# Attention on one core: the values of the unit behind are multiplied between the two pairs of scores

## The chip, the cores and the metric

The kernel runs on one core of a Trainium2 chip. The metric is the device time of one execution in microseconds (us), lower is better. The kernel before takes 2456.95 us, the median of three runs (2456.72 to 2460.13).

## The reference

Two layers act on x of 2 x 2048 tokens with 256 channels. The change is in the attention of the first layer, which has 16 heads of 16 channels and is causal. Cut to what matters:

```
Qr = rope(h @ W_q.T), Kr = rope(h @ W_k.T), V = h @ W_v.T      # per head
scores  = einsum('bhqd,bhkd->bhqk', Qr, Kr) * DH ** -0.5
scores  = where(causal, finfo.min, scores)
pattern = softmax(scores, axis=-1)
heads   = einsum('bhqk,bhkd->bhqd', pattern, Vh)
out     = heads.transpose(0, 2, 1, 3).reshape(b, t, d) @ W_o.T
```

Before it stand a layer norm and the projections, behind it a gated sum, a top-1 expert layer, a second layer with a Toeplitz mix, and a routed expert layer. None of these is touched.

## The kernel before, in words

The program runs its parts one after the other: `projections`, `attention`, `output_projection`, `top1_experts`, `layer1`, `routed_experts`, `combine`. Each has one instruction stream for each engine, written out by hand, with semaphores between them. TensorE works through its stream in the order written: an instruction that waits holds up all behind it.

**Stages and units.** Attention has 8 stages of 4 heads each. A stage has 40 units (c, j): c is a chunk of 512 queries (0 to 3), j a block of 128 keys, up to the diagonal (4(c+1) blocks for chunk c). The units with j >= 4c, 16 of the 40, are on the diagonal; their first columns are left out (`lo`), so their four heads are 512, 384, 256 and 128 queries wide in turn. The 24 others are full, 512 wide. Unit numbers n run from 0 to 39 here; chunks begin at n = 0, 4, 12 and 24, diagonal units are n = 0 to 3, 8 to 11, 20 to 23 and 36 to 39.

For a unit the engines do this:

- TensorE, `scores` (line 819): for each head h one matmul, keys by queries, into one of three banks `p_s` (NSCORES = 3, line 608). It waits until the exponential three places earlier has been taken out of its bank.
- ScalarE (ACT), `exponentials` (line 914): one exponential for each head, from `p_s` to `probs`, which has room for three units.
- GpSimd (POOL), `mask` (line 770): on a diagonal unit, zeroes the upper half of a 128x128 block of each head, once its exponential is done; `diag_masked` is raised behind the fourth.
- TensorE, `values` (line 833): four matmuls of 32 rows of output each, one a head, which add values times `probs` into `p_o`. It first waits for the fourth exponential of its unit, or on the diagonal for the fourth mask. At j = 0 it also waits for `o_taken`, since `p_o` starts anew: ACT copies the finished chunk out (`take_o`, line 920), behind the four exponentials of the new chunk's first unit.

**Maxima.** The softmax needs row maxima, found one stage ahead by separate matmuls (`maximum_products`, lines 216 and 219): 80 maxima in a stage, each of two heads, for a 128-query tile and up to 512 keys, into one of two places `p_m`; on the diagonal each of the two matmuls is followed by a small one that adds the mask. VectorE (DVE) reduces them (line 227). A maximum waits until the reduction two before it is done. The table MAXIMA (line 653) says how many maxima of the next piece go behind the first pair of scores of each unit and how many behind the second, for example (2, 1) or (1, 0): 18 units of 40 have none behind their second pair, 20 have one, 2 have two. Behind units 5, 19, 23 and 31 TensorE turns finished maxima into rows (line 842), and behind the fourth unit of each chunk (j = 3) it turns an output chunk (line 849), which DVE then divides (lines 975 and 977). The last stage has no next one, so its maxima end with unit 17.

**Order on TensorE** (`stage`, line 852): for each unit, scores of heads 0 and 1; the maxima of this place; scores of heads 2 and 3; the values of the unit behind (n - 1); the maxima of this place. The unit behind unit 0 is the last one of the stage before. The code shown next has these functions.

Of the kernel before, what the change touches and what calls it, by code (L numbers as in the profile page):

```python
# [91 lines left out]
def first(i):  # L92
    return isinstance(i, int) and i == 0
# [504 lines left out]
def attention(nc, a, k):  # L598
# [7 lines left out]
    with ExitStack() as stack:  # L606
# [71 lines left out]
        def maxima_of(n, pair, more):  # L678

            u0 = 2 * MAX_LEAD + sum(map(sum, MAXIMA[:n])) + (MAXIMA[n][0] if pair else 0)  # L680
            return [u for u in range(u0, u0 + MAXIMA[n][pair]) if u < NMAX or more]

        def maxima_turned_at(s, n, more):

            c, following = TURN_MAXIMA.get(n, (None, False))
            if c is None or following and not more:
                return None
            return (s + 1 if following else s), c

        def output_at(s, n):  # L690

            c, j = units[n]
            if j != AFTER_TURN_O or not c and first(s):
                return None
            return (s, c - 1) if c else (s - 1, CPS - 1)
# [12 lines left out]
        def m_bank(x):  # L708

            return M_AT[x] % 2  # L710

        def s_bank(x, buf):

            return (M_SHIFT * buf + S_AT[x]) % NSCORES
# [3 lines left out]
        def wait_m_bank(pe, s, x, more):  # L718

            i = M_AT[x] - 2  # L720
            if i < 0:
                what, which = M_ORDER[i]
                which -= NMAX if what == "max" else CPS
                if first(s):
                    what, which = "max", 2 * MAX_LEAD + i
            else:
                what, which = M_ORDER[i]
            if first(s) and (what, which) == ("out", -1):
                what, which = M_ORDER[i - 2]
            if not more and what == "max" and which >= NMAX:  # L730
                while what == "max" and which >= NMAX:
                    i -= 2
                    what, which = M_ORDER[i]
            if what == "max":
                pe.wait_ge(k.max_taken, NMAX * s + which + 1)
            else:
                pe.wait_ge(att_ready, CPS * s + which + 2)

        def wait_s_bank(pe, s, x, more):

            i = S_AT[x] - NSCORES
            if i < 0 and first(s):
                if i + NSCORES < 2:
                    pe.wait_ge(max_rows_ready, i + NSCORES + 1)
                return
            if not more and S_ORDER[i][0] == "rows" and S_ORDER[i][1] >= CPS:
                i -= NSCORES
            what, which = S_ORDER[i]
            if what == "rows":
                pe.wait_ge(max_rows_ready, CPS * (s if i >= 0 else s - 1) + which + 1)  # L750
            else:
                pe.wait_ge(probs_ready, HG * UNITS * s + which + 1 - (0 if i >= 0 else HG * UNITS))

        with nc.Block(no_gpsimd_drain=True) as block:
# [55 lines left out]
            def _(pe):  # L810
                def maximum(s, buf, u, at_bank):
                    maximum_products(nc, k, qa[buf], ka[buf], u, p_m[:, at_bank, :, :]).then_inc(k.max_scores, 1)

                def scores(s, buf, n, h, more):
                    c, j = units[n]
                    lo = max(0, j - TPC * c) * P
                    x = ("exp", HG * n + h)
                    wait_s_bank(pe, s, x, more)
                    nc.tensor.matmul(p_s[:, s_bank(x, buf), lo:CH], ka[buf][0:QROWS + SPLIT, h, j * P:(j + 1) * P],  # L819
                                     qa[buf][0:QROWS + SPLIT, h, c * CH + lo:(c + 1) * CH],  # L820
                                     start=True, stop=True).then_inc(scores_ready, 1)

                def values(s, buf, n):
                    c, j = units[n]
                    lo = max(0, j - TPC * c) * P
                    if n in diag_no:
                        pe.wait_ge(diag_masked, DIAGS * s + diag_no[n] + 1)
                    else:
                        pe.wait_ge(probs_ready, HG * (UNITS * s + n) + HG)
                    if j == 0 and (c or not first(s)):  # L830
                        pe.wait_ge(o_taken, CPS * s + c)
                    for h in range(HG):
                        last = nc.tensor.matmul(p_o[VW * h:VW * (h + 1), lo:CH], va[buf][:, j, VW * h:VW * (h + 1)],  # L833
                                                probs[:, (buf * UNITS + n) % NPROBS, h, lo:CH], start=j == 0, stop=j == TPC * (c + 1) - 1)
                    last.then_inc(probs_used, 1)

                def turn_maxima(n, at_bank):

                    pe.wait_ge(max_parts_ready, n + 1)
                    rows = p_s[:, at_bank, :].bitcast(BF16)  # L840
                    for i in range(TPC):
                        last = nc.tensor.transpose(rows[0:SPLIT * HG, i * P:(i + 1) * P],
                                                   max_parts[:, i, :, :].rearrange("p s h -> p (s h)"), k.identb[:, :])
                    last.then_inc(max_turned, 1)

                def turn_outputs(s, c, at_bank):
                    pe.wait_ge(o_taken, CPS * s + c + 1)
                    for u in range(TPC):
                        last = nc.tensor.transpose(p_m[:, at_bank, 0, u * P:(u + 1) * P], o_sb[:, u * P:(u + 1) * P],
                                                   k.ident[:, :])  # L850
                    last.then_inc(o_turned, 1)

                def stage(s, buf, more, loads):
                    nbuf = (buf + 1) % NBUF
                    for n, (c, j) in enumerate(units):
                        if j == 0:
                            pe.wait_ge(max_placed[c % 2], PLACED * (CPS // 2 * s + c // 2 + 1))
                            if c == 0 and not first(s):
                                pe.wait_ge(ones_set, NBUF - 1)
                        for pair in range(2):  # L860
                            scores(s, buf, n, 2 * pair, more)
                            scores(s, buf, n, 2 * pair + 1, more)
                            if pair:

                                if n:
                                    values(s, buf, n - 1)
                                elif not first(s):
                                    values(s - 1, (buf - 1) % NBUF, UNITS - 1)
                            for u in maxima_of(n, pair, more):
                                if u == NMAX:  # L870
                                    pe.wait_ge(stage_loaded[nbuf], 16 * LOADS * loads)
                                wait_m_bank(pe, s, ("max", u), more)
                                if u < NMAX:
                                    maximum(s, buf, u, m_bank(("max", u)))
                                else:
                                    maximum(s + 1, nbuf, u - NMAX, m_bank(("max", u)))
                        turned = maxima_turned_at(s, n, more)
                        if turned:
                            x = ("rows", CPS * TURN_MAXIMA[n][1] + TURN_MAXIMA[n][0])
                            wait_s_bank(pe, s, x, more)  # L880
                            turn_maxima(CPS * turned[0] + turned[1], s_bank(x, buf))
                        out = output_at(s, n)
                        if out:
                            x = ("out", c - 1)
                            wait_m_bank(pe, s, x, more)
                            turn_outputs(*out, m_bank(x))

                pe.wait_ge(k.stage0_loaded, 16 * LOADS)
                for u in range(EARLY, 2 * MAX_LEAD):
# [7 lines left out]
                    if ends_chunk(u):  # L897
                        turn_maxima(MAX_UNITS[u][0], MAX_UNITS[u][0])
                all_stages(pe, stage)
                values(NS - 1, (NS - 1) % NBUF, UNITS - 1)  # L900
                pe.wait_ge(att_ready, CPS * NS)
# [1642 lines left out]
```

## Time and profile before

| | |
|---|---|
| median of the runs | 2456.95 us |
| the profiled execution | 2465.7 us |
| its span, from first to last instruction | 2464.0 us |
| attention's units in it | about 225 to 1095 us |
| TensorE matmuls busy, whole span | 2207.4 us (90%) |
| VectorE, ScalarE, GpSimd busy | 1713.8, 1273.3, 877.2 us |
| exponentials, line 914, ScalarE | 1280, 596.4 us busy |
| reductions, line 227, VectorE | 628, 642.0 us busy |
| matmuls of values, line 833 | 2560 records, 301.8 us |
| matmuls of scores, line 819 | 1280 records, 352.0 us |

How to read it: a matmul's record lasts from its start to the end of its result, and the next one starts before that. So TensorE's busy time says that something was in it, not that it was full; what a step costs TensorE is the distance between the start of its first matmul and the start of what follows. A timeline line merges neighbours of one kind (x4) and starts at the first.

### The profile page before, as it was taken

To read this page: it belongs to the slowest core of one execution; us is meant where nothing else is said; L and a number is where in the kernel's file an instruction comes from. 1 tells how busy PE (TensorE), PEld (TensorE's weight loads), DVE (VectorE), ACT (ScalarE), POOL (GpSimd) and SP (SyncE) were. 2 spreads that over 40 slices of the span, in tenths; PEclk is the share of its full clock that TensorE was granted. 3 is DMA by queue.
4 is the path that set the end of the run, shared out by engine and by line. 5 is a ranking of instruction groups with operands and counts; after the bars stand their busy time and mean duration, and the time that the engine had idled before them with its cause. 6 is when DMAs were issued, how large, how long until landed. Compare 5 with 4: busy or idle time off the path is not lost. (4 is left out here: it accounts for less than half of the span.)

```text
span 2464.0 us, 38748 instructions
## 1 busy us (share of the span) xinstructions
PE 2207.4 (90%) x12968; PEld 1401.7 (57%) x12968; DVE 1713.8 (70%) x2750; ACT 1273.3 (52%) x2452; POOL 877.2 (36%) x1057
## 2 busy tenths in 40 slices
PE   7878999999999999979999599962999999999991
PEld 5752333333333333326777456642888888888881
DVE  8968787878788787816888778764455555555566
ACT  3332777777677777773333344421555555555552
POOL 4542321313121220213555413444345444445350
PEclk9986999999999999998999798875999999999996
DMA  6499004225050500012000100004544434444326
GB/s 211 141 209 120 19 8 64 35 37 70 3 70 2 70 2 2 1 58 76 0 0 0 34 1 18 35 33 158 180 142 138 144 133 137 169 157 142 133 74 218
DMA packets 129541, 199.84 MB, mean 81 GB/s; under 512 B 13712, under 2 KB 102416, under 8 KB 127952
## 3 DMA queue, kind: packets, MB, share of 16 engines
q1 hardware_dynamic: 112992, 143.93, 17.5%
q0 software_dynamic: 14544, 48.05, 10.9%
q10 hardware_dynamic: 1824, 5.52, 1.3%
q8 instruction: 105, 1.72, 0.3%
q14 instruction: 76, 0.62, 0.1%
HBM read 150.58 MB, written 46.49 MB: 80 GB/s over the span
## 5 line engine op out<-in xcount | busy, mean ns | idle before, releaser
L227 DVE TENSOR_REDUCE tile_max<-p_m 128x2 f32<-128x1024 f32 (+1 forms) x628 | 642.0, 1064 | 135.9 <-PE p_m L219 67.9
L914 ACT ACTIVATE probs<-p_s 128x512 f32<-128x512 f32 (+3 forms) x1280 | 596.4, 534 | 241.3 <-PE p_s L819 236.1
L2180 PE MATMUL p_up<-f_xT,f_w 128*128 128x512 f32 (+1 forms) x2304 | 464.4, 351 | 12.1 <-POOL f_w L2345 8.6
L2180 PEld LDWEIGHTS p_up<-f_xT,f_w 128*128 128x128 f32 x2304 | 368.6, 189 | 64.7 <-issue 14.3
L770 POOL TENSOR_SCALAR_AFFINE_SELECT probs<-probs 128x128 f32<-128x128 f32 x512 | 145.9, 294 | 700.8 <-ACT probs L914 692.2
L2345 POOL TENSOR_TENSOR f_w<-f_raw,f_w 128x1024 fp32r<-128x1024 f32 x96 | 233.3, 2437 | 374.4 <-ACT f_w L2233 374.4
L819 PE MATMUL p_s<-qa,ka 99*128 99x512 bf16 (+3 forms) x1280 | 352.0, 351 | 13.0 <-ACT probs L914 7.2
L216 PE MATMUL p_m<-ka,qa 96*128 96x512 bf16 (+1 forms) x1256 | 352.9, 363 | 11.1 <-DVE tile_max L227 5.0
L833 PE MATMUL p_o<-probs,va 128*32 128x512 f32 (+3 forms) x2560 | 301.8, 542 | 1.2 <-issue 0.9
L2195 PE MATMUL p_y<-f_w,f_hidden 128*128 128x256 f32 x1872 | 252.9, 281 | 15.0 <-DVE f_y L2307 14.1
L2195 PEld LDWEIGHTS p_y<-f_w,f_hidden 128*128 128x128 f32 x1872 | 238.1, 188 | 29.8 <-issue 21.6
L216 PEld LDWEIGHTS p_m<-ka,qa 96*128 96x128 bf16 x1256 | 108.2, 99 | 237.3 <-DVE tile_max L227 137.1
L2294 DVE SCALAR_TENSOR_TENSOR f_gate<-p_up,f_b,f_gate 128x512 f32<-128x512 f32 (+1 forms) x192 | 124.6, 649 | 168.3 <-ACT f_gate L2246 165.8
L819 PEld LDWEIGHTS p_s<-qa,ka 99*128 99x128 bf16 x1280 | 110.5, 98 | 223.3 <-ACT probs L914 141.5
L2298 DVE TENSOR_TENSOR f_hidden<-f_gate,f_hidden 128x512 fp32r<-128x512 f32 (+1 forms) x192 | 141.3, 736 | 118.7 <-ACT f_hidden L2251 110.8
L2246 ACT ACTIVATE f_gate<-p_up,f_b 128x512 f32<-128x512 f32 (+1 forms) x192 | 116.3, 606 | 155.5 <-PE p_up L2180 148.7
L1268 PE MATMUL p_e<-w_expert,c_hT 128*128 128x512 f32 x768 | 195.0, 404 | 0.0
L2251 ACT ACTIVATE f_hidden<-f_gate 128x512 fp32r<-128x512 f32 (+1 forms) x192 | 105.9, 552 | 159.9 <-DVE f_gate L2294 156.6
L1268 PEld LDWEIGHTS p_e<-w_expert,c_hT 128*128 128x128 f32 x768 | 140.6, 190 | 29.5
L2233 ACT ACTIVATE f_w<-f_raw 128x1024 fp32r<-128x1024 f32 x144 | 150.4, 1045 | 5.8 <-DMA f_raw<-in_W1b 3.9
L1706 PE MATMUL p_uv<-l_xnT,w_uv 128*128 128x512 f32 x256 | 112.8, 597 | 0.0
L536 PE MATMUL p_qk<-hT,wqkv 128*128 128x512 f32 x384 | 97.3, 413 | 13.0 <-DVE rot L397 13.0
(279 smaller groups left out, 2622.3 us busy)
## 6 DMA issues: line engine op xcount, KB each, us to landing
f_raw<-in_W1a SPq DMA_DIRECT2D x24, 1024.0 KB, 6.5
f_raw<-in_W1b SPq DMA_DIRECT2D x24, 1024.0 KB, 8.7
f_raw<-in_W SPq DMA_DIRECT2D x24, 1024.0 KB, 11.1
qk_scr<-parts SPq DMA_DIRECT2D x48, 256.0 KB, 2.8
qa<-qk_scr POOLq DMA_DIRECT2D x42, 256.0 KB, 15.9
ka<-qk_scr POOLq DMA_DIRECT2D x42, 256.0 KB, 17.6
v_scr<-wqkv_raw SPq DMA_DIRECT2D x32, 256.0 KB, 3.8
g_ys<-y_rows SPq DMA_DIRECT2D x16, 512.0 KB, 8.8
```

Of the source, the lines that this page charges most:

```text
L216: last = nc.tensor.matmul(out[:, hh, 0:width], qa[0:QROWS, hd, q0:q0 + P], ka[0:QROWS, hd, bank * CH:bank * CH + width], start=True, stop= ...
L227: return nc.vector.tensor_reduce(out=k.tile_max[:, 2 * hp:2 * hp + 2, i, bank], in_=products[:, :, 0:width], op=ALU.max, axis=AX.X)
L770: last = nc.gpsimd.affine_select(block_, block_, pattern=[[1, P]], compare_op=ALU.is_ge, fill=0.0, base=0, channel_multiplier=-1)
L819: nc.tensor.matmul(p_s[:, s_bank(x, buf), lo:CH], ka[buf][0:QROWS + SPLIT, h, j * P:(j + 1) * P], qa[buf][0:QROWS + SPLIT, h, c * CH + lo: ...
L833: last = nc.tensor.matmul(p_o[VW * h:VW * (h + 1), lo:CH], va[buf][:, j, VW * h:VW * (h + 1)], probs[:, (buf * UNITS + n) % NPROBS, h, lo: ...
L914: nc.scalar.activation(probs[:, (buf * UNITS + n) % NPROBS, h, lo:CH], p_s[:, s_bank(("exp", HG * n + h), buf), lo:CH], ACT.Exp, scale=DH ...
L1268: last = nc.tensor.matmul(out, hT[:, par, hp, kt, :], weights(wp, kt), start=(kt, wp, hp) == (0, HI, HI), stop=(kt, wp, hp) == (KT - 1, LO ...
L2180: last = nc.tensor.matmul(p_up[:, f % 2, ab, 0:size], w1[:, wh, ab * KT + kt, f * P:(f + 1) * P], xT[:, t % 2, xh, kt, 0:size], start=(kt, ...
L2195: last = nc.tensor.matmul(p_y[:, u, :], hidden[:, (FB * t + f) % NHID, hh, u * P:(u + 1) * P], w2[:, wh, f, :], start=(f, wh, hh) == (0, H ...
L2233: nc.scalar.activation(piece_part(q, HI), piece_raw(q, par), ACT.Copy).then_inc(w_high, 1)
L2298: nc.vector.tensor_tensor(hidden[:, (n - 1) % NHID, LO, 0:size], gate[:, f % 2, 0:size], hidden[:, (n - 1) % NHID, HI, 0:size], ALU.subtra ...
L2345: nc.gpsimd.tensor_tensor(piece_part(q, LO), piece_raw(q, t % 2), piece_part(q, HI), ALU.subtract).then_inc(w1_ready, 1)
```

## The change

In `stage` of TensorE's stream one condition is turned round. `values(n - 1)` stands behind the first pair of scores of unit n, ahead of the maxima of the first place, and no longer behind the second pair. Nothing is added or removed, and the streams of the other engines are the same.

```diff
@@ -860,7 +860,7 @@
                         for pair in range(2):
                             scores(s, buf, n, 2 * pair, more)
                             scores(s, buf, n, 2 * pair + 1, more)
-                            if pair:
+                            if not pair:
 
                                 if n:
                                     values(s, buf, n - 1)
```

**First place, TensorE, on the diagonal of chunk 1 in the first stage** (units 9 to 11, second pair of unit 9 to second pair of unit 11). p_s is scores, p_o values, p_m maxima. Before:

```order
L819 MATMUL p_s<-qa,ka 128x384 x2
L833 MATMUL p_o<-probs,va 32x512 x4
L819 MATMUL p_s<-qa,ka 128x256 x2
L216 MATMUL p_m<-ka,qa 128x512 x4
L819 MATMUL p_s<-qa,ka 128x256 x2
L833 MATMUL p_o<-probs,va 32x384 x4
L819 MATMUL p_s<-qa,ka 128x128 x2
L216 MATMUL p_m<-ka,qa 128x512 x2
L819 MATMUL p_s<-qa,ka 128x128 x2
L833 MATMUL p_o<-probs,va 32x256 x4
```

Now:

```order
L819 MATMUL p_s<-qa,ka 128x384 x2
L819 MATMUL p_s<-qa,ka 128x256 x2
L833 MATMUL p_o<-probs,va 32x384 x4
L216 MATMUL p_m<-ka,qa 128x512 x4
L819 MATMUL p_s<-qa,ka 128x256 x2
L819 MATMUL p_s<-qa,ka 128x128 x2
L833 MATMUL p_o<-probs,va 32x256 x4
L216 MATMUL p_m<-ka,qa 128x512 x2
L819 MATMUL p_s<-qa,ka 128x128 x2
```

The 384-wide values of unit 9 stood behind four matmuls of scores of unit 10 and its maxima; now they stand behind its first pair, which follows at once on the second pair of unit 9, since this unit has no maxima in its second place.

**Second place, TensorE, at the start of chunk 2** (from the first pair of unit 12; the four-in-a-row of scores are the second pair of one unit and the first of the next). Before:

```order
L819 MATMUL p_s<-qa,ka 128x512 x2
L216 MATMUL p_m<-ka,qa 128x512 x2
L819 MATMUL p_s<-qa,ka 128x512 x2
L833 MATMUL p_o<-probs,va 32x128 x4
L819 MATMUL p_s<-qa,ka 128x512 x2
L216 MATMUL p_m<-ka,qa 128x512 x2
L216 MATMUL p_m<-ka,qa 128x384
L219 MATMUL p_m<-masks,identb 128x128
L216 MATMUL p_m<-ka,qa 128x384
L219 MATMUL p_m<-masks,identb 128x128
L819 MATMUL p_s<-qa,ka 128x512 x2
L833 MATMUL p_o<-probs,va 32x512 x4
```

Now:

```order
L819 MATMUL p_s<-qa,ka 128x512 x2
L833 MATMUL p_o<-probs,va 32x128 x4
L216 MATMUL p_m<-ka,qa 128x512 x2
L819 MATMUL p_s<-qa,ka 128x512 x4
L833 MATMUL p_o<-probs,va 32x512 x4
L216 MATMUL p_m<-ka,qa 128x512 x2
L216 MATMUL p_m<-ka,qa 128x384
L219 MATMUL p_m<-masks,identb 128x128
L216 MATMUL p_m<-ka,qa 128x384
L219 MATMUL p_m<-masks,identb 128x128
L819 MATMUL p_s<-qa,ka 128x512 x4
L833 MATMUL p_o<-probs,va 32x512 x4
```

The values of unit 12 are the last line of the first piece, behind both pairs of unit 13 with its maxima between. In the second piece they are the fifth line, and only the first pair of unit 13 lies between the second pair of unit 12 and them; the last line there is the values of unit 13.

## Rows read from the trace of the kernel before

**Rows 1.** Busy time by stretch: attention, a stage's start, the last stage's tail

```profile
core 0: us, PE busy (x) PEld busy (x) DVE busy (x) ACT busy (x) POOL busy (x), PEclk, DMA share, GB/s
225.00:1095.00 870.00, 849.57 (x5746) 304.91 (x5744) 664.45 (x818) 622.74 (x1341) 192.16 (x579) 0.99 0.21 30
660.00:670.00 10.00, 5.90 (x33) 2.09 (x32) 4.72 (x5) 3.08 (x9) 1.96 (x7) 0.70 0.04 9
1064.00:1074.00 10.00, 8.73 (x52) 2.21 (x51) 4.88 (x10) 7.96 (x16) 0.00 (x0) 1.00 0.01 2
```

**Rows 2.** Timeline, two full units: start, us, engine, line, work, count, [idle before, releaser]

```profile
596.58 0.60 PE L819 MATMUL p_s<-qa,ka 99*128 99x512 bf16 x2
596.99 1.09 ACT L914 ACTIVATE probs<-p_s 128x512 f32<-128x512 f32 x2 [0.53 <-PE p_s L819]
597.10 1.06 PE L833 MATMUL p_o<-probs,va 128*32 128x512 f32 x8
598.10 0.61 PE L216 MATMUL p_m<-ka,qa 96*128 96x512 bf16 x2
598.54 0.60 PE L819 MATMUL p_s<-qa,ka 99*128 99x512 bf16 x2
598.75 2.36 DVE L227 TENSOR_REDUCE tile_max<-p_m 128x2 f32<-128x1024 f32 x2 [0.36 <-PE p_m L216]
...
599.53 0.59 PE L819 MATMUL p_s<-qa,ka 99*128 99x512 bf16 x2
```

**Rows 3.** Timeline, TensorE: the transpositions between two units

```profile
573.71 0.66 PE L849 MATMUL p_m<-ident,o_sb 128*128 128x128 f32 x4
...
574.20 0.60 PE L819 MATMUL p_s<-qa,ka 99*128 99x512 bf16 x2
...
639.87 0.60 PE L216 MATMUL p_m<-ka,qa 96*128 96x512 bf16 x2
...
640.73 0.60 PE L819 MATMUL p_s<-qa,ka 99*128 99x512 bf16 x2
```

**Rows 4.** Timeline, TensorE: the values of a 256-wide unit and what follows

```profile
582.94 0.64 PE L833 MATMUL p_o<-probs,va 128*32 128x256 f32 x8
...
583.51 0.60 PE L216 MATMUL p_m<-ka,qa 96*128 96x512 bf16 x2
```

**Rows 5.** Timeline, TensorE: start of the second stage and of the fifth

```profile
335.12 0.60 PE L819 MATMUL p_s<-qa,ka 99*128 99x512 bf16 x2
...
665.69 1.03 PE L819 MATMUL p_s<-qa,ka 99*128 99x512 bf16 x2 [4.10 <-issue]
```

**Rows 6.** Timeline: the last stage's tail, which has no maxima

```profile
1047.06 1.06 PE L833 MATMUL p_o<-probs,va 128*32 128x512 f32 x8
...
1071.75 0.82 PE L819 MATMUL p_s<-qa,ka 99*128 99x512 bf16 x3
1072.23 2.06 ACT L914 ACTIVATE probs<-p_s 128x512 f32<-128x512 f32 x4 [0.39 <-PE p_s L819]
1072.88 0.39 PE L819 MATMUL p_s<-qa,ka 99*128 99x512 bf16 x1 [0.32 <-ACT probs L914]
1073.20 1.07 PE L833 MATMUL p_o<-probs,va 128*32 128x512 f32 x8
...
1094.76 0.43 PE L833 MATMUL p_o<-probs,va 128*32 128x128 f32 x8 [0.30 <-POOL probs L770]
```

**Rows 7.** Groups by shape, attention: the exponentials of a 128-wide unit

```profile
L914 ACT ACTIVATE probs<-p_s 128x128 f32<-128x128 f32 x128 | 28.5, 275 | 19.2 <-PE p_s L819 16.5
```

**Rows 8.** Timeline: what follows a unit's exponentials, on POOL and on ACT

```profile
584.37 2.06 ACT L914 ACTIVATE probs<-p_s 128x512 f32<-128x512 f32 x4 [0.94 <-PE p_s L819]
...
586.29 0.63 ACT L920 ACTIVATE o_sb<-p_o 128x512 f32<-128x512 f32 x1
...
607.74 2.24 ACT L914 ACTIVATE probs<-p_s 128x512 f32<-128x512 f32 x4
...
610.05 0.29 POOL L770 TENSOR_SCALAR_AFFINE_SELECT probs<-probs 128x128 f32<-128x128 f32 x1 [0.19 <-ACT probs L914]
```

## The prediction

> **What bounds the kernel now.** I read the busy time by stretch first [rows 1]. Attention's units take 870 us, and in them TensorE's records cover 849.6 us, VectorE's 664.5, ScalarE's 622.7, at a granted clock of 0.99, so at the upper of TensorE's two levels, 2.4 GHz. Only TensorE can be the bound. But a record outlives its turn, so I go on to the timeline of TensorE and measure distances between starts [rows 2]. A pair of 512-wide scores, alone, costs 0.44 us; before values it costs 0.53 (596.58 to 597.10), so values cost a lead of 0.1; the four matmuls of values cost 1.00 (597.10 to 598.10); an unmasked maximum 0.44 (598.10 to 598.54); pair and masked maximum together 0.99 (598.54 to 599.53), so the masked one 0.55. Turning an output costs 0.49 (573.71 to 574.20); turning maxima 0.42, which is 639.87 to 640.73 less a maximum [rows 3].
>
> I price a whole stage with these. Scores and maxima scale with their width (384, 256 and 128 columns), and of values the 256-wide ones cost 0.57 [rows 4], so about 0.785 and 0.355 at 384 and 128. Scores: 28 units of 0.88 and 4 each of 0.66, 0.44 and 0.22 make 29.9 us. Values with their lead: 28 x 1.10 + 4 x (0.885 + 0.67 + 0.455) = 38.8. Maxima: 48 unmasked at 0.44 and 8 each at 0.55, 0.44, 0.33 and 0.22 make 33.4. Transpositions: 4 x 0.42 + 4 x 0.49 = 3.6 (one output a chunk). Sum 105.8 us. A stage lasts (665.69 - 4.10 - 335.12) / 3 = 108.8 us [rows 5]; the 4.10 is the idle time at the loop's turn. So TensorE is full but for 3.0 us a stage, and **any wait that the new order puts in front of it costs its full length**.
>
> **What the change does.** Work and its amount stay. Moved are 319 calls of values (40 a stage, but for the one behind the last unit), each past one pair of scores and the maxima of the first place. No transfer is moved, and no instruction of another engine. What changes is how much TensorE has to do between the second pair of scores of unit n and values(n), which needs all four exponentials of that unit. Before: first pair and maxima of unit n + 1, and its second pair too, and the second pair's wait for a bank already covers the fourth exponential. Now: the maxima behind n's second pair and one pair.
>
> **How long the exponentials take.** From the start of the second pair to the end of its second exponential: 0.41 (596.58 to 596.99) plus 1.09 for the two [rows 2], so 1.50. From there to a waiting matmul 0.06: in the tail the first of four exponentials starts at 1072.23, takes 0.60 (two take 1.09, four 2.06, so each further one adds 0.49) and so ends at 1072.83 and the waiting score starts at 1072.88 [rows 6]. So **values(n) can start 1.56 us after the second pair** of a full unit. Narrower ones: a 128-wide exponential takes 0.275 [rows 7] against 0.60, so two take about 0.44, and by straight line 0.66 and 0.87 at 256 and 384; the 0.41 falls to 0.28, 0.32 and 0.37 by the columns streamed. On the diagonal the mask follows: exponentials end at 609.98, the mask at 610.34, 0.36 more [rows 8]. That makes 1.92, 1.66, 1.40 and 1.14 us for 512, 384, 256 and 128.
>
> **What covers it.** Second pair 0.44, maxima behind it, next first pair 0.44, lead 0.1: 0.98 for a full unit without maxima there, 1.42 with one. The wait is the difference.
> - Full units (24): five without maxima or transposition (12, 13, 28, 30, 34) wait 0.58, 2.9 together; nine with 0.44 us of maxima (4, 6, 14, 16, 24, 26, 32, 33, 35) 0.14, 1.3; 18, 25 and 19 wait 0.36, 0.25 and 0.16; 7, 15 and 27, where an output is turned, 0.09 each; 17 and 29 0.03; 5 and 31 nothing. Sum **5.3**.
> - Diagonal units (16): unit 8 1.05; the 384-wide 1, 9, 21 1.01 each (1.66 less 0.33 + 0.22 + 0.1); the 256-wide 2, 10, 22 0.97 each; 0 and 20 0.50 each, 36 to 39 with 0.61, 0.57, 0.53 and 0.49; 11 0.05; 3 and 23 nothing. Sum **10.2**.
> - A wait that the diff does not show: values at j = 0 also need `o_taken`. ACT copies the output behind the fourth exponential and ends 0.49 us after it (586.92 against 586.43) [rows 8]. So units 0, 4, 12 and 24 come at 1.50 + 0.49 + 0.06 = 2.05: 0.13 more for unit 0 and 0.49 for the three others. Sum **1.6**.
> - The maxima: two in the first place and one in the second now have only 0.44 us of scores between them, since the values have gone. The first is reduced 0.65 + 1.18 us after it starts [rows 2], so the third may start at 1.89 and is ready at 0.88 + 0.44 = 1.32, 0.57 late. Where values would wait anyhow, part of it is hidden: 0.43 more at units 6, 16, 33, 0.57 at 31, 0.54 at 29, 0.2 at 14. Sum **2.6**. In return the values now stand between a turned output and the next maximum, which had waited for VectorE's division. That belongs to the 3.0 us of now, which I let go entirely.
>
> New stage: 105.8 + 5.3 + 10.2 + 1.6 + 2.6 = 125.5, so **+16.7 us**, seven times 117. Last stage: its first 18 units take their part, 7.5 + 1.1 + 1.0 less 18/40 of 3.0, +8.3. Then there are no maxima, and the time from values(18) to values(39) is 47.7 us now (1047.06 to 1094.76) [rows 6]. The new period is the exponentials' time plus the values': 13 x 1.56 + 0.49 + 2 x (1.92 + 1.66 + 1.40 + 1.14) for units 19 to 39, and 19.1 of values, 52.1 us: +4.4. At the first units of stages 1 and 5 TensorE runs at the lower level (0.70 granted in the mean of that stretch, 1.03 for two scores against 0.60 [rows 1, 5]), where its own work covers unit 0's wait: -1. Total 117 + 8.3 + 4.4 - 1 = **+129 us**. The profiled execution of 2465.7 us would take 2595; against the median, 2456.95, I forecast **2586 us**.
>
> The unknown sizes. The 0.41 was 0.48 in the tail (1071.75 to 1072.23) [rows 6]: on some 35 waits in 8 stages up to +20. The maxima's term lies between nothing (-20) and twice (+20). Without the wait for `o_taken`, -13. So 2553 to 2626.
>
> **The rivals.**
> 1. *Only long waits count.* The 0.09 to 0.58 of full units are no waits, because TensorE would be held up by VectorE in that same place whatever the order: DVE's reductions, 1.18 each, two a unit, are the next longest. Then diagonal and `o_taken` remain, (10.2 + 1.6 - 3.0) x 8 = +70: 2527 us. Against it: VectorE is busy only 76% of the stretch [rows 1].
> 2. *The clock falls.* With a wait in most units, TensorE might be granted the lower level for part of the time. If for a tenth, its work doubles there: 0.1 x 8 x 105.8 = +85, of which waits cover 0.1 x 8 x 19.7 = 16: +69, 2655 us. Against it the tail: TensorE waits there in every unit of 2.45 us for a bank (0.32 of it idle by its records), and the clock is 1.00 [rows 1, 6]. The Trainium skill (TensorE: Matmul & The Clock Gate, section "A second HAM failure mode: psum-queue depth-cycling") says that short, frequent idling of TensorE between groups of matmuls while it cycles through PSUM banks makes the clock swing between its levels. By that rule this rival would be the likeliest; this trace does not agree, with its 1.00.
> 3. *Faster.* The exponentials are done when values come up, and the 3.0 us a stage of present waits go, for values now part the turned output from the next maximum: -24, 2433 us. It decides at 0.98 us from second pair to last exponential. For it: probabilities come free earlier. Against it: two exponentials alone take 1.09 [rows 2].
> 4. *No difference.* The order is the same where it counts, or TensorE isn't the bound. The instructions' order above says that each call moved; the length of a stage against the sum of its work says that it is full [rows 5]: 2457 us.
>
> **How the numbers follow.** The forecast has 0.77, rival 1 0.09, rival 2 0.07, rival 3 0.04, rival 4 0.03. A range of 2525 to 2626 us takes in the forecast's bounds and rival 1 and leaves out the rest, with a little for sizes that I have missed. A measurement of this kernel can tell about 0.2%, 5 us. Faster 0.04, the same 0.03, slower 0.93.
>
> **What would show it.** In the profile of the changed kernel, TensorE's weight loads or matmuls of values (line 833) must wait for ScalarE (line 914), on the diagonal for POOL (line 770) and at chunk starts for the output copy (line 920), where before there was next to nothing; a stage must last about 125 us; distances from second pair to values must be 1.56 on full and 1.92 on 512-wide diagonal units; work between stays at 105.8. VectorE's and ScalarE's busy time must not change. The forecast is wrong if stages last under 115 us, if values start sooner than 1.5 us after the second pair, or if the granted clock in attention falls below 0.97.

## The result and the profile after

The changed kernel takes 2615.29 us (median of four, 2609.84 to 2618.61) against 2458.54 us of the kernel before beside it: a ratio of 1.0622, 95% interval 1.0599 to 1.0644, **156.8 us slower**. Forecast were 2586 us and +129. The profiled execution took 2618.59 us.

Nearly all of it lies in attention. The last values of the last stage start at 1246.04 us, before at 1094.76 [rows 6], 151.3 later, and the two profiled executions differ by 152.9 us (2618.59 against 2465.7). The first scores start at 225.63 in the changed kernel and at 225.66 before, so attention, from first scores to last values, takes 1020.4 us against 869.1. The same stretches as in [rows 1], columns as there: all of attention, a full stretch, the last stage's tail.

```profile
core 0: us, PE busy (x) PEld busy (x) DVE busy (x) ACT busy (x) POOL busy (x), PEclk, DMA share, GB/s
225.00:1246.00 1021.00, 887.08 (x5738) 302.49 (x5736) 667.45 (x818) 619.29 (x1341) 189.65 (x579) 0.99 0.18 25
340.00:440.00 100.00, 87.05 (x587) 31.14 (x588) 68.46 (x85) 60.06 (x136) 24.46 (x77) 1.00 0.32 43
1160.00:1240.00 80.00, 66.78 (x407) 18.62 (x407) 27.50 (x37) 56.21 (x119) 10.13 (x36) 1.00 0.00 1
```

VectorE's and ScalarE's busy time is what it was (664.5 and 622.7 in [rows 1]), the granted clock 0.99 as before. TensorE's records no longer fill the time. Where the second and the fifth stage start:

```profile
353.98 0.98 PE L819 MATMUL p_s<-qa,ka 99*128 99x128 bf16 x4
...
743.47 1.03 PE L819 MATMUL p_s<-qa,ka 99*128 99x512 bf16 x2 [3.46 <-issue]
```

The first row holds two pairs that merge: the last of the first stage, 128 wide and 0.11 us by the prediction's costs, and the first of the second stage, which so starts at 354.09. A stage lasts (743.47 - 3.46 - 354.09) / 3 = 128.6 us, against 108.8 before [rows 5] and 125.5 forecast. The view of the waits over attention's stretch says on whom TensorE now waits (engine and line, for whom, us in total, times, longest). PE are its matmuls; PEld are its weight loads. These overlap running matmuls (at 886.84 us one row of 0.32 us starts under matmuls that last from 886.61 to 887.21), so their waits cost time only in part:

```profile
PEld p_m L216 <- DVE tile_max L227: 185.8, 249, 0.9
...
PEld p_o L833 <- POOL probs L770: 70.9, 124, 0.8
PEld p_o L833 <- ACT probs L914: 63.1, 130, 0.9
PE p_o L833 <- POOL probs L770: 37.7, 88, 0.5
PE p_m L216 <- DVE tile_max L227: 33.3, 77, 0.7
PE p_s L819 <- ACT probs L914: 32.9, 117, 0.5
...
PE p_o L833 <- ACT o_sb L920: 13.1, 23, 0.7
```

In the same view of the kernel before:

```profile
PEld p_m L216 <- DVE tile_max L227: 115.4, 193, 1.9
...
PEld p_o L833 <- ACT probs L914: 31.3, 76, 0.4
...
PE p_s L819 <- ACT probs L914: 7.2, 21, 0.6
...
PE p_m L216 <- DVE tile_max L227: 1.4, 6, 0.3
...
PE p_o L833 <- POOL probs L770: 0.3, 1, 0.3
```

The three new waits of the prediction are there, for the exponentials (914), the masks (770) and the output copy (920). So is one that it had priced far too low: maxima behind VectorE's reductions.

These sums count idle time between records only, and a record outlasts its turn. So I used the prediction's way on the whole of attention: from every start on TensorE to the next, less the cost that the prediction gives to that work, put down to what starts next. (From 236 us on; the loop's turn and some 3 us before the transpositions of the maxima are left out.) In us:

| next is | before | changed | difference |
|---|---|---|---|
| a score (bank of `p_s`) | 15.7 | 48.7 | +33 |
| values | 4.3 | 83.1 | +79 |
| a maximum (place in `p_m`) | 15.9 | 52.9 | +37 |

The sum of work by the same costs is 817.6 and 818.9 us, so the differences, 149 us, are nearly all of the 151. With the same work on both sides the waits have to add up to the time lost; what the table adds is where they stand. A single entry depends on how finely the work is priced. If each of the two scores of a pair is put at half of the pair, 0.22 us at full width, the rows read 21.7, -2.1 and 14.3 before and 55.8, 74.6 and 52.3 changed: entries move by up to 9 us, the differences (34, 77, 38) by no more than 2. Below, "the account" means the counting of the table.

**The distances, one by one.** The timeline of TensorE from 902 us on, a 512-wide, a 384-wide and a 256-wide diagonal unit and, from 917.39, a full one; the x3 rows are the second pair and the first score of the next unit:

```profile
902.07 0.76 PE L819 MATMUL p_s<-qa,ka 99*128 99x512 bf16 x3
903.14 0.34 PE L819 MATMUL p_s<-qa,ka 99*128 99x384 bf16 x1 [0.31 <-ACT probs L914]
903.99 1.07 PE L833 MATMUL p_o<-probs,va 128*32 128x512 f32 x8 [0.51 <-POOL probs L770]
...
905.67 0.60 PE L819 MATMUL p_s<-qa,ka 99*128 99x384 bf16 x3
...
907.32 0.85 PE L833 MATMUL p_o<-probs,va 128*32 128x384 f32 x8 [0.46 <-POOL probs L770]
...
908.98 0.44 PE L819 MATMUL p_s<-qa,ka 99*128 99x256 bf16 x3
...
910.36 0.64 PE L833 MATMUL p_o<-probs,va 128*32 128x256 f32 x8 [0.41 <-POOL probs L770]
...
917.39 0.81 PE L819 MATMUL p_s<-qa,ka 99*128 99x512 bf16 x3
...
918.46 0.39 PE L819 MATMUL p_s<-qa,ka 99*128 99x512 bf16 x1 [0.26 <-ACT probs L914]
918.95 1.06 PE L833 MATMUL p_o<-probs,va 128*32 128x512 f32 x8
```

From second pair to values: 1.92, 1.65, 1.38 and 1.56 us, where the prediction had 1.92, 1.66, 1.40 and 1.56. The same units give the same distances, within 0.02, in all eight stages; the 128-wide units 3 and 11, not shown, come at 1.19, where it had 1.14. The row at 918.46 shows that the wait comes in two parts: the second score of the next unit's first pair first waits for its bank (1.07 us from 917.39, ready at 0.66), and only then the values for the fourth exponential.

### The profile page after: what moved, and what is told of

Its sections match the earlier page's. It is cut to its first block and busy times, and to the rows that moved or that the text cites. A ratio compares the mean times of both kernels' runs of the same rounds, so it can differ in the third digit from the quotient of the medians.

```text
span 2616.9 us, 38748 instructions
## 1 busy us (share of the span) xinstructions
PE 2244.7 (86%) x12968; PEld 1399.5 (53%) x12968; DVE 1717.0 (66%) x2750; ACT 1269.5 (49%) x2452; POOL 874.3 (33%) x1057
## 5 line engine op out<-in xcount | busy, mean ns | idle before, releaser
L216 PEld LDWEIGHTS p_m<-ka,qa 96*128 96x128 bf16 x1256 | 101.0, 99 | 354.6 <-DVE tile_max L227 207.5
L819 PEld LDWEIGHTS p_s<-qa,ka 99*128 99x128 bf16 x1280 | 116.0, 98 | 209.2 <-ACT probs L914 116.5
L833 PEld LDWEIGHTS p_o<-probs,va 128*32 128x32 f32 x2560 | 51.6, 108 | 162.0 <-POOL probs L770 72.0
```

What stands on the lines that cost most here:

```text
L216: last = nc.tensor.matmul(out[:, hh, 0:width], qa[0:QROWS, hd, q0:q0 + P], ka[0:QROWS, hd, bank * CH:bank * CH + width], start=True, stop= ...
```

## The experiments

All times are medians; "above" is the difference to the kernel before on the same chip, 2463.84 us for the first eight runs and 2461.37 us for the last four. The changed kernel stands 156.8 above. The interval of a ratio reaches some 0.2% to either side, 5 us, so differences of 10 or 15 us between two experiments are rough; for these the length of attention in the trace, from first scores to last values (1020.4 us in the changed kernel), stands beside them.

**1. Values two units behind, in the same place.**

```diff
-                                if n:
-                                    values(s, buf, n - 1)
-                                elif not first(s):
-                                    values(s - 1, (buf - 1) % NBUF, UNITS - 1)
+                                if n >= 2:
+                                    values(s, buf, n - 2)
+                                elif not first(s):
+                                    values(s - 1, (buf - 1) % NBUF, UNITS - 2 + n)
...
-        AFTER_O, AFTER_TURN_O = 0, 3
+        AFTER_O, AFTER_TURN_O = 1, 3
```

> The change as it is, but between the two pairs of scores of unit n stand the values of unit n - 2, not n - 1 (the copy of a finished chunk on ACT moves one unit back with it). The place is the same; what is gone is the need to wait for exponentials just issued. Theory A (TensorE waits at the values for exponentials, masks and the output copy, 17 us a stage; the rest is maxima standing too close together, which stays): a stage falls from 128.4 to about 111 us and the time to 2470 us, 2460 to 2490. Theory B (the place between the pairs is bad in itself, since it feeds ScalarE and VectorE unevenly): it stays near the changed kernel, over 2580 us. Theory C (the clock falls from the waits): the granted clock of the attention's stages in the changed kernel would be under 0.97, and here 1.00.

Measured: 2547.89 us, ratio 1.0343 (1.0322 to 1.0364), 84 above. The wait for exponentials goes, as the distances say: by the same account values fall from 83.1 to 21.0 us, and the rest of these is the copy of a finished chunk, which this edit puts just ahead of its reader. But I had expected 2470. The waits at scores stay (47.9) and those at maxima too (52.3). The timeline of this kernel at the place of the first rows above:

```profile
616.31 0.76 PE L819 MATMUL p_s<-qa,ka 99*128 99x512 bf16 x3
617.38 0.34 PE L819 MATMUL p_s<-qa,ka 99*128 99x384 bf16 x1 [0.31 <-ACT probs L915]
617.65 1.07 PE L833 MATMUL p_o<-probs,va 128*32 128x512 f32 x8
```

The values start 1.34 us after the second pair, not 1.92; the bank's wait, 1.07 us from the second pair to the fourth score in a row, is unchanged. With three banks the last of four full scores in a row waits here, whatever stands behind it. So of 157 us the values' own wait is not the whole; two neighbours of the move cost as well.

**2. and 3. No causal mask, in either order.** POOL's `affine_select` is taken out and the values wait for the fourth exponential.

```diff
-                    if n in diag_no:
-                        pe.wait_ge(diag_masked, DIAGS * s + diag_no[n] + 1)
-                    else:
-                        pe.wait_ge(probs_ready, HG * (UNITS * s + n) + HG)
+                    pe.wait_ge(probs_ready, HG * (UNITS * s + n) + HG)
```

> The changed kernel without the causal mask on the diagonal blocks: POOL masks nothing, and the values of diagonal units wait for the fourth exponential like all others. Left out is the masking of 4 blocks in each of 128 units. Theory A: 0.36 us less at every diagonal unit that waits and is not a chunk's first behind the copy, 4.4 us a stage, 35 us in all: 2580 us (2573 to 2590). Theory B: no difference, since TensorE's place does not depend on the mask.

> The kernel before without the causal mask on the diagonal blocks (left out is the masking of 4 blocks in each of 128 units). Control for the mask's share: in this order both pairs of scores and a place of maxima stand between a mask's exponential and the values, so its 0.36 us lie hidden. Theory A: within 5 us of the kernel before. If the mask costs something in itself, 30 us less here too.

Measured: in the changed order 2583.47 us, 119.6 above, so 37 us gone (35 expected; attention is 31.2 us shorter in the trace), and by the account 34 at the values (83.1 to 49.3). In the order before 2461.76 us, ratio 0.9996 (0.9986 to 1.0005): nothing. The mask's 0.36 us cost only where they stand in front of TensorE.

**4. The copy between the second and third exponential.**

```diff
-                        exponentials(s, buf, n)
+                        exponentials(s, buf, n, range(0, 2))
                         if j == AFTER_O and c:
                             take_o(s, c - 1, n - 1)
                         elif j == AFTER_O and not first(s):
                             take_o(s - 1, CPS - 1, UNITS - 1)
+                        exponentials(s, buf, n, range(2, HG))
```

> The changed kernel, but ACT copies the finished output chunk between the second and third exponential of a chunk's first unit, not behind the fourth. Theory A: the values of units 4, 12, 24 and 0 no longer wait for the copy, which took 0.49 us of them and 0.13 of unit 0: 1.6 us a stage, 13 us in all, 2602 us (2598 to 2608). If the copy there delays the third exponential, less. Theory B: no difference, or slower.

Measured: 2606.31 us, 142.5 above, 14 us gone (13 expected). The intervals of this ratio (1.0561 to 1.0602) and the changed kernel's just touch, so its size rests on the traces: attention is 13.1 us shorter, and values fall from 83.1 to 71.4 in the account. The hidden wait for `o_taken` was real and had about its size.

**5. Values behind the maxima of the first place.** The call of `values` stands after the loop over `maxima_of(n, 0, more)`.

> The values of the unit behind still between the pairs, but behind the maxima of the first place, not ahead of them. Theory A: the maxima of the first place (0.44 to 0.88 us) now cover the exponentials too; waits by the same sum fall from 17.1 to 4.4 us a stage, and the third maximum of a (2, 1) unit has the values ahead of it again, so the 5.5 us of maxima waits mostly go: a stage of 112 to 114 us, 2490 us (2478 to 2505). Theory B: no nearer to the kernel before than half of the loss, over 2540 us.

Measured: 2521.22 us, ratio 1.0225 (1.0198 to 1.0251), 57.4 above, where I expected 26. Values' waits fall to 13.6 and maxima's to 23.9 (13.7 with single scores at 0.22 us), both as meant. Scores' stay at 48.1: the maxima now cover the values, but not the bank of the score before them. That is the miss of experiment 1 again, seen from the other side, and at 33 us over the kernel before it is the size of this one. Against the rival that the place itself is bad, over half of the loss is gone.

**6. to 8. One maximum in each place of every unit**, in the changed order, in the order before, and with values two behind plus the early copy:

```diff
+        MAXIMA = [(1, 1)] * UNITS
```

> The changed kernel with one maximum in each of the two places of every unit, in place of the table's (2, 1), (1, 0), (1, 2) and so on; the sum of 80 a stage is the same. Theory A (TensorE's waits at the values are the time of exponentials and masks less the work between; waits at the maxima come from three maxima with too little between them): one maximum now stands behind every second pair, so waits at values and scores fall from 17.1 to 11.4 us a stage, about 43 us in all, and the 53 us of waits at maxima that the changed kernel's trace shows fall to some 12: together 80 to 85 us less, 75 us above the kernel before (60 to 90). Rival D (VectorE's reductions pace the maxima wherever they stand): the waits at maxima stay near 50 us, and only 43 us are gained: 115 us above the kernel before.

> The kernel before with one maximum in each place of every unit. A control for the table alone: Theory A has no wait for exponentials here, and maxima already stood apart; the narrow units become paced by the reductions (two of 1.18 us in a unit of 1.8 to 2.2 us). Within 10 us of the kernel before, on either side.

> Values of unit n - 2 between the pairs, one maximum in each place of every unit, and ACT's copy of the finished chunk between the second and third exponential of the unit behind a chunk's first. Theory A: nothing is left to wait for at the values, the second score of the first pair comes 1.10 us after the second pair and its bank is free at 1.08, and the maxima are far enough apart: a stage of 107 us against 108.8 before, and 5 to 25 us faster than the kernel before. Theory B (the place between the pairs is bad in itself): slower than the kernel before by over 30 us. Rival D: slower by some 30 us too, from waits at maxima.

Measured: 2577.78 us (113.9 above, expected 75), 2520.00 us (56.2 above, expected within 10) and 2505.31 us (41.5 above, expected 5 to 25 below). All three are missed. What they share is waiting for reductions: narrow units give TensorE less work than two reductions give VectorE, and the uneven table puts fewer maxima there. In the changed order this is only part of the miss: the values' waits did not shrink either (37.0 us for masks and 17.3 for the copy in its view of the waits, against 37.7 and 13.1); why was not traced. In the order before with the even table, the fourth unit of a chunk's diagonal, in the second stage (first row) and in the fourth:

```profile
355.21 0.61 PE L216 MATMUL p_m<-ka,qa 96*128 96x512 bf16 x2 [1.44 <-DVE tile_max L227]
...
584.13 0.28 PE L820 MATMUL p_s<-qa,ka 99*128 99x128 bf16 x2
585.98 0.61 PE L216 MATMUL p_m<-ka,qa 96*128 96x512 bf16 x2 [1.57 <-DVE tile_max L227]
...
590.00 1.06 PE L216 MATMUL p_m<-ka,qa 96*128 96x512 bf16 x2
...
598.64 0.60 PE L216 MATMUL p_m<-ka,qa 96*128 96x512 bf16 x2
```

In the fourth stage TensorE idles 1.57 us, and what follows runs at half its rate (1.06 for two, not 0.61) until about 598. The stretches of 5 us, that behind 355.21 first:

```profile
355.00:360.00 5.00, 4.28 (x33) 1.70 (x34) 4.83 (x7) 1.99 (x6) 0.54 (x2) 1.00 0.01 5
...
580.00:585.00 5.00, 4.41 (x34) 1.53 (x31) 4.08 (x9) 2.95 (x9) 2.58 (x10) 1.00 0.00 0
585.00:590.00 5.00, 3.75 (x21) 1.74 (x22) 4.68 (x6) 0.63 (x3) 0.80 (x4) 0.75 0.01 2
590.00:595.00 5.00, 5.00 (x23) 1.82 (x21) 2.98 (x4) 3.61 (x7) 0.00 (x0) 0.50 0.01 3
```

The granted clock falls to 0.50, the lower level, here. TensorE idles 1.2 to 1.6 us in one piece fifteen times in this attention, nearly twice a stage; behind six of them the clock fell, for some 3 to 10 us each (near 240, 471, 587, 714, 833 and 949 us), and behind nine, that at 355 among them, it did not. (It falls near 700 us too, but that is the loop's turn, as in every kernel here.) By the granted clock of the stretches of 5 us the six make some 37 us at half rate. My estimate from that is up to 19 us lost, so perhaps a third of the 56 us is the clock's.

This bears on the comparison among the three. With the even table and nothing to wait for at the values, the place between the pairs takes 2505 us and the place before 2520. But from 236 us to attention's end the granted clock is 1.00 in the mean for the first and 0.98 for the second, and the 15 us are no more than the clock may have cost. So the place between the pairs is shown to be no worse in itself; that it is better is not shown.

The changed order with the even table has two such falls as well, of some 3 us each, and in the 10 us ahead of each no single idle time of the matmuls is over 0.61 us. The second one:

```profile
979.66 0.61 PE L216 MATMUL p_m<-ka,qa 96*128 96x512 bf16 x2 [0.41 <-DVE tile_max L227]
980.79 1.12 PE L850 MATMUL p_m<-ident,o_sb 128*128 128x128 f32 x4 [0.52 <-DVE tile_max L227]
...
975.00:980.00 5.00, 3.91 (x30) 1.44 (x30) 4.63 (x9) 1.71 (x7) 2.05 (x8) 1.00 0.01 3
980.00:985.00 5.00, 4.48 (x23) 1.90 (x21) 3.21 (x5) 1.54 (x3) 0.11 (x1) 0.66 0.02 3
```

**9. Two of the late third maxima relieved.**

```diff
+        MAXIMA[5], MAXIMA[7], MAXIMA[32], MAXIMA[34] = [(1, 1)] * 4
```

> The changed kernel with four entries of the table altered: units 5 and 32 from (1, 2) to (1, 1), units 7 and 34 from (1, 0) to (1, 1). The trace of the changed kernel shows units 5 and 32 late at their third maximum (by 0.83 and 0.69 us), which must wait for the reduction of a full one two before it, and units 6 and 33 by 0.43. Theory A': these waits go, since no three maxima with a full one first stand together there, and units 7 and 34 get 0.44 us more to cover their exponentials: 2.7 us a stage, some 20 us less than the changed kernel, 137 us above the kernel before (130 to 145). Theory D (reductions pace the maxima wherever they stand): no gain, 150 us or more above.

Measured: 2603.30 us, 141.9 above, 15 less than the changed kernel (20 expected; attention is 11.1 us shorter in the trace); maxima's waits 52.9 to 32.2 in the account. That the reductions set a pace of their own wherever the maxima stand is refuted for this kernel.

**10. The two numbers of every unit exchanged.**

```diff
+        MAXIMA = [(second, one) for one, second in MAXIMA]
```

> The changed kernel with the two numbers of every unit exchanged, so that the heavier place, 1 or 2 maxima, is behind the second pair and the lighter between values and second pair. Theory A: cover rises by 0.44 us or more nearly everywhere: waits at values and scores 7.1 in place of 17.1 us a stage by the sum of the prediction; waits at maxima stay, since three still stand with only 0.44 us of scores among them (4 to 6 us a stage). 60 to 85 us less than the changed kernel, 85 us above the kernel before (70 to 100). Theory B (the place is bad in itself): no gain of over 20 us.

Measured: 2550.96 us, ratio 1.0360 (1.0343 to 1.0378), 89.6 above (85 expected), 67 less than the changed kernel. Scores' waits fall to 6.8 (a maximum now parts the two pairs nearly everywhere), values' to 52.6, maxima's are 60.7. What covers an exponential is the work between the second pair and the values; more of it there means less waiting.

**11. and 12. Short reductions**, at most 256 columns read, in either order.

```diff
-    return nc.vector.tensor_reduce(out=..., in_=products[:, :, 0:width],
+    return nc.vector.tensor_reduce(out=..., in_=products[:, :, 0:min(width, 256)],
```

> The changed kernel with reductions that read at most 256 of a maximum's columns, so VectorE takes about 0.69 us and not 1.22 for a full one. Left out is the maximum over the other columns. Theory A: the 53 us of waits at maxima go almost wholly, some 8 to 12 us come back as waits at the values that they had hidden, all other waits stay: 40 to 45 us less, 115 us above the kernel before (105 to 125), which is what exponentials, masks and the copy alone cost. Rival: if the waits at values only mirror late maxima, they go too, and it comes within 60 us of the kernel before.

> The kernel before with the same short reductions (same part left out). Control: its trace has 16 us of waits at maxima, about half behind VectorE's division and so not touched: 6 to 16 us faster than the kernel before.

Measured: 2571.54 us, 110.2 above, and 2445.46 us, 15.9 below (ratio 0.9938, 0.9921 to 0.9955). Maxima's waits are 12.2 and 9.9 in the account; scores and values in the changed order have 139.8, 8 more than with the full reductions, which hid them. The difference of the two, 126 us, is what exponentials, masks, copy and banks cost by themselves; by the medians 157 - 126 = 31 us of the loss are the maxima's. In the traces attention takes 989.7 and 859.5 us, 130.2 apart, so it is 151.3 - 130.2 = 21 us there. (Some 7 of the 15.9 us lie ahead of attention's units: the first scores start at 218.58 us with short reductions and at 225.66 without.)

No kernel here beats the kernel before with all its work done.

## Why the prediction was right

**Right: what bounds, and that waits add.** TensorE had 3.0 us of slack a stage, and the moved calls meet it with their full length: 149 us of new waits, 151 us of time. VectorE, ScalarE and the clock did what they did before.

**Right: the exponentials' time and its cover.** The distances of 1.56, 1.92, 1.66 and 1.40 us were measured to 0.02; the 1.14 of 128-wide units came at 1.19 and the 2.05 of a chunk's first unit at 2.14. The terms of full units, diagonal units and `o_taken` and the last stage's tail came to 5.3 + 10.2 + 1.6 = 17.1 us a stage and, with the last stage's 8.6 and 4.4 and the -1, to 132 us; with maxima out of the way the runs give 126 by the medians and 130 by the traces. The mask's share (35 against 37) and the copy's (13 against 14) hold one by one. The prediction put all of this down to the values; the account shows some 30% of it, 33 of 112 us, at the bank of the score ahead of them. In the kernel as changed that should make no difference, since the values would wait the same time anyway (argued, not tried with a fourth bank), but in experiments 1 and 5 it did, and there my expectations failed by it.

**Mis-sized: the maxima.** "2.6 us" a stage less "the 3.0 us of now, which I let go entirely" gave a term of nearly nothing, -3 us. It measured +31 us by the medians, +21 by the traces and +37 by the account, where part of a wait only replaces another. That is 24 to 34 us more than the term; less the 2 to 6 us by which the other terms were too high, it is the missing 28 us (22 by the traces). The waits at maxima in the changed kernel, 52.9 us in all, lie above the upper bound of "twice" too, 2 x 2.6 x 8 = 42 us; the time stayed within the range because the bounds of other terms were not used up. Three places were left out. First, I looked for three maxima with two in front, and not at the (1, 2) units, 5 and 32, where a full maximum stands ahead of two small ones. Unit 5 of the sixth stage:

```profile
890.19 0.60 PE L216 MATMUL p_m<-ka,qa 96*128 96x512 bf16 x2
890.63 0.60 PE L819 MATMUL p_s<-qa,ka 99*128 99x512 bf16 x2
...
892.12 0.23 PE L216 MATMUL p_m<-ka,qa 96*128 96x128 bf16 x1 [0.66 <-DVE tile_max L227]
```

The third starts 1.93 us after the first, as the prediction's own 0.65 + 1.18 + 0.06 would have it (1.89); the work between is only 1.10. Second, behind the output turned at unit 3 the values are 128 wide and take 0.36 us, so they don't part it from unit 4's maxima, which still wait for the division:

```profile
885.85 0.60 PE L216 MATMUL p_m<-ka,qa 96*128 96x512 bf16 x2
886.13 0.42 DVE L977 TENSOR_TENSOR x<-p_m,recip 128x256 f32 x1 [0.24 <-DVE recip L975]
...
886.61 0.60 PE L216 MATMUL p_m<-ka,qa 96*128 96x512 bf16 x2 [0.16 <-DVE x L977]
```

That wait pushes on the reductions and then unit 4's third maximum (887.77). Third, the 3.0 us of slack were no single thing that could go: part of it may be rounding in my costs. Experiment 9 takes units 5 and 32 out (and gives units 7 and 34 more cover) and gets 15 us back, 11 in the trace; experiments 11 and 12 give the whole.

**The rivals.** Only long waits count: no, unit 13's 0.58 is there in full (from 917.39, 1.56 against 0.98), and 2527 us is far off. The clock falls: not here; TensorE's matmuls idle in 233 of the 320 units and no stretch of 10 us was below 0.99 but at attention's start, at the loop's turn and in its last 10 us. In the changed kernel the Trainium skill's rule (TensorE: Matmul & The Clock Gate, section "A second HAM failure mode: psum-queue depth-cycling"), that frequent short idling between groups makes the clock swing, is not borne out. It is not refuted either: in the changed order with the even table the clock fell twice to the lower level behind idle times of 0.2 to 0.6 us that stood close together. Faster, or no difference: refuted by the ratio.

## What to carry to other kernels

Before a step is moved forward in an in-order queue, take the time from its last input's issue to that input's release (here 1.56 to 2.05 us) and lay beside it the work that would stand between; the difference is paid at every call when the engine is full. Then do the same for everything the moved step had kept apart: here values had parted two pairs of scores from each other (three banks for four scores) and the second maximum from the third (two places), and these two neighbours account for 33 and 37 us of waits. A table of counts fitted to one order is not a free choice: evened out, it cost 56 us in the order before, perhaps a third of it through the clock.

## What the runs showed of the hardware

- In the changed kernel TensorE's matmuls stood idle for 0.1 to 0.7 us in 233 of attention's 320 units (and for 3.46 us at the loop's turn), its records covering 87% of a stretch (87.05 of 100 us) and 83% of one in the tail (66.8 of 80 us), and the granted clock was 1.00 in both. With the even table idle times of 1.2 to 1.6 us in one piece were followed by 3 to 10 us at the lower level six times out of fifteen, and idle times of up to 0.61 us close together twice in the changed order. So the longest idle time alone does not tell these apart.
- Behind ScalarE's copy of the output a waiting matmul started later than behind an exponential or a mask: 0.15 us (copy 914.76 + 0.60 = 915.36, values at 915.51; the median of 31 copies is the same) against 0.05 to 0.06. So units at a chunk's start came at 2.14 us (913.37 to 915.51) and not at 2.05. Why was not tried.

```profile
913.37 0.81 PE L819 MATMUL p_s<-qa,ka 99*128 99x512 bf16 x3
...
914.76 0.60 ACT L920 ACTIVATE o_sb<-p_o 128x512 f32<-128x512 f32 x1
...
915.51 1.06 PE L833 MATMUL p_o<-probs,va 128*32 128x512 f32 x8 [0.68 <-ACT o_sb L920]
```
